# Two of four heads transposed by VectorE and sixteen transfers a group, in groups 2 to 9 of a two-layer graph kernel

## The chip, the core and the metric

One core of one Trainium2 chip. The metric is the device time of one execution in microseconds; the kernel before has a median of 3792.05 over 3 runs (3787.47 to 3802.44).

## What is computed

Two layers over B = 16 graphs of N = 1024 nodes with D = 256 features, each added to its input. The first is attention with 8 heads of 32 features under an adjacency mask, the second weights nodes by edge scores. Cut to what matters:

```python
h = maximum(layernorm(x), 0)
Q, K, V = proj(Wq, bq), proj(Wk, bk), proj(Wv, bv)          # b, 8 heads, 1024, 32
scores = where(adj == 0, -inf, einsum('bhnd,bhmd->bhnm', Q, K) * SCALE)
x = x + einsum('bhnm,bhmd->bhnd', softmax(scores), V) @ Wo.T + bo
h = maximum(layernorm(x), 0)
e_k = leaky_relu(einsum('bid,bjd->bij', h * a_k, h))        # k = 0..3, chosen by adj == k + 1
x = x + einsum('bij,bjd->bid', softmax(where(adj == 1, e_0, ...)), h)
```

## The kernel before

A **tile** is one head's scores of 128 nodes against all 1024: 8 heads x 8 blocks of nodes = 64 tiles a graph, numbered t, and four tiles (four heads of the same nodes) are a **group** g = t // 4, 16 groups a graph. The program has one step a tile, the slot s, and every engine walks the 64 slots of a graph in its own `stage` function; the loop over graphs has graph b's first layer and, between its slots, the second layer of graph b - 1 (its "edge" tiles t = 0..7, from slot 13 on, four slots each) and the front of graph b + 1 (from slot 40). Graph 0 is peeled off and has no second layer beside it. The order is written out by hand: `background` gives for each slot what PE does `ahead` of that slot's transposes and `behind` them, and the other engines read the same lists.

A tile goes through: scores on PE (L1070, two matmuls into `ps`), mask with row minimum on DVE (L754, into `sm`, a ring of three buffers), exponential on ACT (L490), eight 128x128 transposes on PE (L1082, into `pT[0]` and `pT[1]`), and a half copy each on ACT (L501) and DVE (L766) into `pt`, so that the other nodes lie on the partitions. When a group's four tiles are there, the value product (L1095, "av") multiplies them with `v` in 32 matmuls (64 records in the trace), ACT copies the result to `ot` (L511). The lookahead is fixed: PE does the scores of tile s + 3 in slot s, after waiting for the mask of tile s + 1; DVE does the mask of tile s + 2 in slot s, before it copies tile s:

```python
pe.wait_ge(masked, TILES * b + s + 2)      # PE, slot s, then scores(b, s + 3)
behind[HG * g + HG].append(("av", g))      # the value product of group g: slot 4g + 4
```

The second layer uses the same engines: matmuls for edge scores (L1017), masks (L865), leaky ReLU (L873), transposes (L1143), copies (L551, L881), the product (L1152) and the result (L886, L889). SP issues all transfers from one queue, in order: the adjacency halves (L230), which POOL turns into masks, the stores (L274), x (L218, L221) and the "stacks" (L250), which copy 32 partitions of `parts` into `qs` or `ks` of three row blocks, 128 KB each, twelve in a row.

## Time and profile before

| | |
|---|---|
| Median of 3 runs | 3792.05 us (3787.47 to 3802.44) |
| Span of the profiled execution | 3783.3 us; its own time isn't given apart from it |
| PE, PEld | 3454.1 us (91%), 2916.1 us (77%) |
| DVE, ACT, POOL | 75%, 65%, 30% |
| Chain that ended last | PE 61%, issue 11%, ACT 10%, SPq 7%, DVE 7% |
| DMA | 286.63 MB on SP's queue, 27.0% of 16 engines |

PE is the matmul side of TensorE and PEld its weight loads, which overlap; a busy PE is not PE at its peak, since matmuls are pipelined. The chain is followed back from the last instruction to whatever released each step; "issue" is time in which the engine waited for nothing that the profile shows. SPq is SP's queue of DMA instructions.

### The profile page before, as it was taken

The numbers are of one execution on the slowest core, as the hardware profiler recorded it, in microseconds if no ns is written. First come the engines' busy times: TensorE is split into PE (matmuls) and PEld (weight loads), VectorE is DVE, ScalarE is ACT, GpSimd is POOL, SyncE is SP. The second block draws the span as 40 slices with busy tenths as digits, with TensorE's granted clock in tenths as the row PEclk, the third lists the DMA queues.
The fourth block names the chain that finished last, engine by engine and source line by source line (L and its number), as shares of the span: only waits on it lengthen the run. The fifth ranks groups of instructions, "written<-read, shape, count | busy, mean of one in ns | idle before, by whom it ended". The sixth has DMA issues, their size and how long they took to land.

```text
span 3783.3 us, 97534 instructions
## 1 busy us (share of the span) xinstructions
PE 3454.1 (91%) x34096; PEld 2916.1 (77%) x34096; DVE 2850.7 (75%) x5622; ACT 2464.4 (65%) x4548; POOL 1125.2 (30%) x568
## 2 busy tenths in 40 slices
PE   5889999899998999999899998999989999998975
PEld 4678778787787878778787787877878787787864
DVE  4777778787787878878777787878778787887752
ACT  4775767657676676766757676666766757676541
POOL 2232423323232232423323232232422324233212
PEclk8999999999999999999999999999999999999988
DMA  4141412314132141412414132141321414123101
GB/s 120 51 113 54 128 36 81 93 58 122 40 103 72 59 121 55 112 53 67 107 54 128 40 100 75 54 125 49 110 57 56 122 54 128 40 86 89 37 27 44
DMA packets 166740, 294.99 MB, mean 78 GB/s; under 512 B 25536, under 2 KB 75968, under 8 KB 166080
## 3 DMA queue, kind: packets, MB, share of 16 engines
q1 hardware_dynamic: 166080, 286.63, 27.0%
q8 instruction: 361, 5.91, 0.7%
q14 instruction: 299, 2.45, 0.2%
HBM read 169.09 MB, written 16.78 MB: 49 GB/s over the span
## 4 chain that ended last, share of the span: by engine, by line
PE 61%; issue 11%; ACT 10%; SPq 7%; DVE 7%; DMA 2%; POOL 0%; DVEq 0%; ACTq 0%; POOLq 0%
PE pT L1082 15%; PE pG L1017 13%; PE pG L1095 11%; PE pG L1152 8%; PE ps L1070 7%; SPq L250 6%; ACT sm L490 4%; PE pT L1143 3%; PE pG L1051 3%; DMA adj_half<-in_adj_dram 2%; ACT pt L501 2%; DVE sm L754 1%; DVE pt L766 1%; PE pG L1108 1%; ACT sm L546 1%
## 5 line engine op out<-in xcount | busy, mean ns | idle before, releaser
L754 DVE CUSTOM_DVE_ANT_0 sm<-ps,bias 128x1024 f32<-128x1024 f32 x1024 | 1244.1, 1215 | 20.6 <-issue 17.0
L1082 PE MATMUL pT<-ident,sm 128*128 128x128 f32 x8192 | 1099.7, 276 | 127.0 <-ACT pt L501 108.9
L1082 PEld LDWEIGHTS pT<-ident,sm 128*128 128x128 f32 x8192 | 946.5, 141 | 345.0 <-ACT sm L490 140.4
L490 ACT ACTIVATE sm<-sm,mn 128x1024 f32<-128x1024 f32 x1024 | 1180.5, 1153 | 48.5 <-DVE mn L754 48.0
L501 ACT COPY pt<-pT 128x512 f32<-128x512 f32 x1024 | 596.3, 582 | 592.6 <-PE pT L1082 592.4
L766 DVE COPY pt<-pT 128x512 f32<-128x512 f32 x1024 | 703.0, 687 | 287.1 <-PE pT L1082 281.4
L417 POOL TENSOR_SCALAR gbias<-adj_half 128x512 bf16<-128x512 int32 x256 | 505.2, 1973 | 1324.3 <-DVE mn L865 1030.1
L1070 PE MATMUL ps<-ks,qs 96*128 96x512 f32 x2048 | 760.9, 453 | 76.7 <-DVE mn L754 64.1
L400 POOL TENSOR_SCALAR bias<-adj_half 128x512 bf16<-128x512 int32 x256 | 492.5, 1924 | 785.5 <-DMA adj_half<-in_adj_dram 712.0
L1095 PE MATMUL pG<-pt,v 128*32 128x128 f32 x16384 | 530.7, 283 | 27.5 <-DVE x L889 18.5
L1095 PEld LDWEIGHTS pG<-pt,v 128*32 128x32 f32 x16384 | 455.1, 114 | 87.9 <-issue 39.3
L1152 PE MATMUL pG<-h,pt 128*128 128x256 f32 x1920 | 468.6, 379 | 0.0
L1070 PEld LDWEIGHTS ps<-ks,qs 96*128 96x128 f32 x2048 | 350.4, 192 | 146.8 <-DVE mn L754 66.0
L865 DVE CUSTOM_DVE_ANT_0 sm<-pG,gbias 128x512 f32<-128x512 f32 x256 | 176.9, 691 | 280.8 <-PE pG L1017 237.9
L1017 PE MATMUL pG<-hh,parts 128*128 128x512 f32 x1024 | 376.5, 410 | 2.7 <-DVE parts L736 2.7
L1152 PEld LDWEIGHTS pG<-h,pt 128*128 128x128 f32 x1920 | 346.5, 190 | 41.0
L511 ACT COPY ot<-pG 128x128 f32<-128x128 f32 x256 | 68.2, 267 | 353.7 <-PE pG L1095 350.4
L1017 PEld LDWEIGHTS pG<-hh,parts 128*128 128x128 f32 x1024 | 197.4, 193 | 43.2 <-DVE parts L736 3.1
L546 ACT ACTIVATE sm<-sm,mnl 128x1024 f32<-128x1024 f32 x128 | 146.6, 1145 | 92.0 <-DVE mnl L876 90.5
L1017 PE MATMUL pG<-hl,parts 128*128 128x512 f32 x512 | 204.1, 399 | 0.0
L490 ACT ACTIVATION_READ_ACCUMULATOR sm<-sm,mn 128x1 f32 x1024 | 198.5, 194 | 0.0
L1143 PE MATMUL pT<-ident,sm 128*128 128x128 f32 x1024 | 145.4, 287 | 42.2 <-ACT sm L546 37.9
(104 smaller groups left out, 3328.1 us busy)
## 6 DMA issues: line engine op xcount, KB each, us to landing
adj_half<-in_adj_dram SPq DMA_DIRECT2D x512, 256.0 KB, 2.9
ks<-parts SPq DMA_DIRECT2D x384, 128.0 KB, 2.4
qs<-parts SPq DMA_DIRECT2D x384, 128.0 KB, 2.6
x<-in_x_dram SPq DMA_DIRECT2D x16, 1024.0 KB, 5.6
out_dram<-x SPq DMA_DIRECT2D x128, 128.0 KB, 2.6
x<-in_x_dram SPq DMA_DIRECT2D x32, 256.0 KB, 3.5
rb<-in_x_dram SPq DMA_DIRECT2D x16, 256.0 KB, 3.2
sq<-in_x_dram SPq DMA_DIRECT2D x16, 256.0 KB, 3.3
```

Source lines behind the costliest of these rows:

```text
L400: nc.gpsimd.tensor_scalar(bias[:, node, c * HALF:(c + 1) * HALF], adj_half[:, c, :], 0.0, BIG, ALU.is_equal, ALU.mult).then_inc(adj_used[c ...
L417: nc.gpsimd.tensor_scalar(half, adj_half[:, c, :], 0.5, BIG, ALU.is_lt, ALU.mult).then_inc(adj_used[c], 1)
L490: nc.scalar.activation(sm[:, ring(t), :], sm[:, ring(t), :], ACT.Exp, scale=-1.0, bias=mn[:, t:t + 1], accum_out=den[:, t:t + 1]).then_inc ...
L501: nc.scalar.copy(pt[:, place(t), 0:NT // 2, :], pT[0][:, :].rearrange("p (m n) -> p m n", n=P)).then_inc(pt_made[0], 1)
L754: nc.vector.tensor_tensor_reduce(out=sm[:, ring(t), :], in0=ps[t % 2][:, :], in1=bias[:, node, :], scale=1.0, scalar=3e38, op0=ALU.add, op ...
L766: nc.vector.tensor_copy(pt[:, place(t), NT // 2:, :], pT[1][:, :].rearrange("p (m n) -> p m n", n=P)).then_inc(pt_made[1], 1)
L1017: last = nc.tensor.matmul(out, a, c, start=start and i == 0, stop=stop and i == len(terms) - 1)
L1070: last = nc.tensor.matmul(ps[t % 2][:, c * HALF:(c + 1) * HALF], qs[0:ROWS, head, node * P:(node + 1) * P], ks[:, head, c * HALF:(c + 1) * ...
L1082: last = nc.tensor.transpose(pT[c][:, j * P:(j + 1) * P], sm[:, ring(t), m * P:(m + 1) * P], ident[:, :])
L1095: last = nc.tensor.matmul(pG[i][HD * h:HD * (h + 1), 0:P], v[:, m, o:o + HD], pt[:, place(HG * g + h), m, :], start=(m == 0), stop=(m == N ...
L1143: last = nc.tensor.transpose(pT[c][:, j * P:(j + 1) * P], sm[:, RING, m * P:(m + 1) * P], ident[:, :])
L1152: last = nc.tensor.matmul(out[:, 0:D], pt[:, edge_place(t), m, :], h1[:, m, :], start=(m == 0), stop=(m == NT - 1))
```

## The change

In groups 2 to 9 the first two tiles of each group are transposed by DVE in blocks of 32x32 (`turn`, into `turned`), and sixteen transfers of 32 partitions and 64 KB (`swap_blocks`) put the blocks on the right partitions of `pt`. PE's transposes and both half copies of these tiles are gone; for the other two tiles of such a group ACT does both half copies. The value product of these groups stands ahead of the transposes in slot 4g + 6 in place of behind them in slot 4g + 4. The buffer `turned` lies over the projection weights, which four transfers park in unused rows of `ks` and bring back once a graph. Around this, `rows`, `norm`, `result`, some edge transposes and products, and the front's statistics move by a slot or a few. Counters of transposes and copies count only the tiles still done by PE (`PLAIN`). Cut to its core (the pieces stand in the order of the file: tables, `background`, SP's new functions and its `stage`, ACT's `copy`, DVE's `turn` and `stage`, PE's `values` and `stage`):

```diff
+SWAPPED = tuple(range(2, 10))
+BATCH = 4 * 16
+TURNED = tuple(HG * g + h for g in SWAPPED for h in range(2))
+PLAIN = tuple(t for t in range(TILES) if t not in TURNED)
...
     for g in range(1, GROUPS - 1):
-        behind[HG * g + HG].append(("av", g))
+        if g in SWAPPED:
+            ahead[HG * g + HG + 2].append(("av", g))
+        else:
+            behind[HG * g + HG].append(("av", g))
...
+            def swap_blocks(b, g):
+                sp.wait_ge(turn_made, len(TURNED) * b + turned_before(HG * g + 2))
+                settle(sp)
+                sp.wait_ge(av, GROUPS * b + g)
+                settle(sp)
+                for k in range(4):
+                    for a in (0, 2, 1, 3):
+                        c = a ^ k
+                        sp.dma_start(swap[HD * c:HD * (c + 1), :, a, :, :].rearrange("p h m j -> p h (m j)"),
+                                     turned[HD * a:HD * (a + 1), :, c, :, :].rearrange("p h m j -> p h (m j)")
+                                     ).then_inc(swapped[a], 16)
...
-                for t in range(4):
-                    edge_adj(o, t, base)
+                edge_adj(o, 0, base)
+                edge_adj(o, 1, base)
+                swap_blocks(b, 2)
+                swap_blocks(b, 3)
+                edge_adj(o, 2, base)
+                swap_blocks(b, 4)
+                edge_adj(o, 3, base)
+                swap_blocks(b, 5)
                 store(o, 0)
                 edge_adj(o, 4, base)
+                swap_blocks(b, 6)
...
+                if t // HG in SWAPPED:
+                    act.wait_ge(tr[1], len(PLAIN) * b + plain_before(t) + 1)
+                    nc.scalar.copy(pt[:, place(t), NT // 2:, :], pT[1][:, :].rearrange("p (m n) -> p m n", n=P)
+                                   ).then_inc(pt_made[1], 1)
...
+            def turn(b, t, first):
+                dve.wait_ge(exped, TILES * b + t + 1)
+                if t == TURNED[0] and first:
+                    dve.wait_ge(parked, BATCH)
+                if t % HG == 0 and (t > TURNED[0] or not first):
+                    for a in range(4):
+                        dve.wait_ge(swapped[a], BATCH * (len(SWAPPED) * b + SWAPPED.index(t // HG)))
+                settle(dve)
+                nc.vector.transpose(turned[:, t % HG, :, :, :].rearrange("p c m j -> p m c j"),
+                                    sm[:, ring(t), :].rearrange("p (m c j) -> p m c j", m=NT, c=4)
+                                    ).then_inc(turn_made, 1)
...
-                    copy(b, s, not earlier)
+                    if s in TURNED:
+                        turn(b, s, not earlier)
+                    elif s // HG not in SWAPPED:
+                        copy(b, s, not earlier)
...
+                if g in SWAPPED:
+                    for a in range(4):
+                        pe.wait_ge(swapped[a], BATCH * (len(SWAPPED) * b + SWAPPED.index(g) + 1))
...
+                        if HG * g + h in TURNED:
+                            moving = swap[:, h, :, m, :]
...
-                    transposes(b, s, not earlier)
+                    if s not in TURNED:
+                        transposes(b, s, not earlier)
```

Three places in the order of the instructions. First DVE in graph 0, slots 15 to 18, before: each slot has a mask (`sm,mn<-ps,bias`) and a half copy; the reciprocal and L777 are row factors, L787 is a norm.

```order
L773 RECIPROCAL rden<-den 128x16 [waits exped]
L777 SCALAR_TENSOR_TENSOR rb<-mn,rden 128x512 [waits f_tr,r_tr,r_rec]
L754 ISA sm,mn<-ps,bias 128x1024 [waits s_mm,tr1]
L754 ISA mn 128x1
L766 COPY pt<-pT 128x512 [waits av,tr1]
L754 ISA sm,mn<-ps,bias 128x1024 [waits s_mm,tr1]
L754 ISA mn 128x1
L787 TENSOR_TENSOR ot<-pG,ot 128x512 [waits r_tr,o_copied]
L766 COPY pt<-pT 128x512 [waits av,tr1]
L754 ISA sm,mn<-ps,bias 128x1024 [waits tr1,adj_used1,s_mm,adj_used0]
```

And DVE in the same slots of the changed program, where tiles 16 and 17 are the first two of group 4.

```order
L896 RECIPROCAL rden<-den 128x16 [waits exped]
L900 SCALAR_TENSOR_TENSOR rb<-mn,rden 128x512 [waits f_tr,r_tr,r_rec]
L864 ISA sm,mn<-ps,bias 128x1024 [waits s_mm,tr1]
L864 ISA mn 128x1
L877 STREAM_TRANSPOSE turned<-sm 128x8x4x32 [waits swapped2,swapped3,swapped1,exped,swapped0]
L864 ISA sm,mn<-ps,bias 128x1024 [waits s_mm,turn_made]
L864 ISA mn 128x1
L877 STREAM_TRANSPOSE turned<-sm 128x8x4x32 [waits exped]
L864 ISA sm,mn<-ps,bias 128x1024 [waits turn_made,adj_used1,s_mm,adj_used0]
```

The half copies are gone; in their place stand two transposes, of which the first waits for the transfers of the group before (`swapped0` to `swapped3`), with the mask of tile 19 behind it. The norm has moved behind a later copy.

Second, PE in graph 0, one group, before: scores (`ps<-ks,qs`) and transposes (`pT<-ident,sm`) in turn, the value product (`pG<-pt,v`) once a group.

```order
L1095 MATMUL pG<-pt,v 32x128 x32
L1070 MATMUL ps<-ks,qs 128x512 x2
L1082 MATMUL pT<-ident,sm 128x128 x8
L1070 MATMUL ps<-ks,qs 128x512 x2
L1082 MATMUL pT<-ident,sm 128x128 x8
L1070 MATMUL ps<-ks,qs 128x512 x2
L1082 MATMUL pT<-ident,sm 128x128 x8
L1070 MATMUL ps<-ks,qs 128x512 x2
L1082 MATMUL pT<-ident,sm 128x128 x8
L1095 MATMUL pG<-pt,v 32x128 x32
```

And a changed group.

```order
L1235 MATMUL pG<-pt,v 32x128 x32
L1215 MATMUL pT<-ident,sm 128x128 x8
L1203 MATMUL ps<-ks,qs 128x512 x2
L1215 MATMUL pT<-ident,sm 128x128 x8
L1203 MATMUL ps<-ks,qs 128x512 x6
L1235 MATMUL pG<-pt,v 32x128 x32
```

Two of four sets of transposes are gone, and the scores of three tiles (x6) stand in a row ahead of the value product, each behind its wait for a mask.

Third, SP in the loop over graphs: between two waits for adjacency halves (`adj_half`) there was nothing or a store.

```order
L230 ISA [waits adj_used1]
L230 DMA adj_half<-in_adj_dram 128x512
L236 ISA
L225 REGISTER_ALU [waits g_sel]
L230 ISA [waits adj_used0]
L230 DMA adj_half<-in_adj_dram 128x512
```

Now:

```order
L277 ISA [waits adj_used1]
L277 DMA adj_half<-in_adj_dram 128x512
L329 REGISTER_ALU
L331 REGISTER_ALU [waits turn_made]
L336 DMA pt<-turned 32x2x256 [waits av]
L336 DMA pt<-turned 32x2x256 x15
```

Sixteen transfers stand behind a wait for the second transpose of their group and for the value product of the group before.

## Rows read from the trace of the kernel before

**Rows 1.** The page, busy time and share of the span by engine.
```profile
PE 3454.1 (91%) x34096; PEld 2916.1 (77%) x34096; DVE 2850.7 (75%) x5622; ACT 2464.4 (65%) x4548; POOL 1125.2 (30%) x568
```

**Rows 2.** Chain of waits, graph 6, one group: start us, us, what.
```profile
1457.91 1.88 PE pG L1095 x64
...
1460.82 0.46 PE ps L1070 x2
...
1462.67 0.87 PE pT L1082 x8
...
1472.40 1.88 PE pG L1095 x64
```

**Rows 3.** Value products 2 and 9 of graph 6, chain of waits, then of graph 0, timeline.
```profile
1430.25 1.88 PE pG L1095 x64
...
1532.68 2.00 PE pG L1095 x64
...
94.26 1.96 PE L1095 MATMUL pG<-pt,v 128*32 128x128 f32 x64
...
162.62 2.01 PE L1095 MATMUL pG<-pt,v 128*32 128x128 f32 x64
```

**Rows 4.** DVE and ACT: costliest groups of the page, then DVE's timeline, graph 6.
```profile
L754 DVE CUSTOM_DVE_ANT_0 sm<-ps,bias 128x1024 f32<-128x1024 f32 x1024 | 1244.1, 1215 | 20.6 <-issue 17.0
L501 ACT COPY pt<-pT 128x512 f32<-128x512 f32 x1024 | 596.3, 582 | 592.6 <-PE pT L1082 592.4
L766 DVE COPY pt<-pT 128x512 f32<-128x512 f32 x1024 | 703.0, 687 | 287.1 <-PE pT L1082 281.4
...
1485.47 0.15 DVE L886 RECIPROCAL rden<-den 128x1 f32<-128x1 f32 x1
...
1486.06 1.21 DVE L754 CUSTOM_DVE_ANT_0 sm<-ps,bias 128x1024 f32<-128x1024 f32 x1
...
1491.87 0.69 DVE L865 CUSTOM_DVE_ANT_0 sm<-pG,gbias 128x512 f32<-128x512 f32 x1 [1.34 <-PE pG L1017]
```

**Rows 5.** SP's queue: durations (ns min/median/max) and landing by line, timeline, the page's queues.
```profile
L250 SPq DMA_DIRECT2D qs<-parts x384: 507/592/2372, 46.4 to 3437.4; - x192
DMA to landing us min/median/max: 2.3/2.4/4.8
L230 SPq DMA_DIRECT2D adj_half<-in_adj_dram x510: 327/333/1552, 33.2 to 3761.0; - x170
L274 SPq DMA_DIRECT2D out_dram<-x x128: 332/356/1200, 312.3 to 3780.4; - x128
...
0.73 0.46 SPq L207 DMA_DIRECT2D x<-in_L_gnn_Wq_dram  x1
1.25 0.45 SPq L207 DMA_DIRECT2D x<-in_L_gnn_Wk_dram  x1
4.74 2.01 SPq L215 DMA_DIRECT2D acol<-in_L_gnn_a_dram  x4
38.59 7.59 SPq L250 DMA_DIRECT2D ks<-parts  x12
1570.57 8.38 SPq L250 DMA_DIRECT2D ks<-parts  x12
q1 hardware_dynamic: 166080, 286.63, 27.0%
```

**Rows 6.** Timeline of graph 6: a result on DVE and the store that waits for it.
```profile
1485.66 0.48 DVE L889 SCALAR_TENSOR_TENSOR x<-pG,rden,x 128x256 f32<-128x256 f32 x1
1486.37 0.35 SPq L274 DMA_DIRECT2D out_dram<-x  x1
```

**Rows 7.** Windows: us, PE, PEld, DVE, ACT, POOL busy (x), granted clock, DMA share, GB/s.
```profile
170.00:200.00 30.00, 20.52 (x221) 16.93 (x222) 16.33 (x28) 18.63 (x37) 7.69 (x4) 0.83 0.22 71
1470.00:1500.00 30.00, 30.00 (x286) 26.21 (x286) 23.00 (x49) 18.35 (x35) 7.84 (x5) 1.00 0.14 47
3700.00:3780.00 80.00, 51.27 (x197) 42.06 (x196) 21.50 (x55) 9.13 (x15) 19.22 (x10) 0.81 0.13 44
```

More of the change, by code:

```diff
@@ L37, with plain_before, turned_before, rows_slot @@
 NORM = {5: (0, 1, 2, 3), 6: (4, 5), 7: (6, 7)}
+def plain_before(t):
+    return sum(1 for p in PLAIN if p < t)
+def turned_before(t):
+    return sum(1 for p in TURNED if p < t)
+def rows_slot(quad):
+    return 16 * quad + (17 if 4 * quad + 3 in SWAPPED else 16)
+def result_slot(t):
+    return EDGE + 1 + 4 * NT if t == NT - 1 else EDGE + (8 if t in LATE else 7) + 4 * t
 def background(earlier, later):
@@ L63, in background @@
         for t in range(NT):
-            behind[EDGE + 4 + 4 * t].append(("sum", t))
+            behind[EDGE + (5 if t in LATE or t == SPARED else 4) + 4 * t].append(("sum", t))
     if later:
@@ L125, in two_graph_layers @@
         xf = [x1[:, 0:2, :], x1[:, 2:4, :]] + [part[:, :].rearrange("p (t d) -> p t d", d=D) for part in (rb, sq)]
-        wqh, wql = sb("wqh", [P, KT, D], R), sb("wql", [P, KT, D], R)
-        wkh, wkl = sb("wkh", [P, KT, D], R), sb("wkl", [P, KT, D], R)
+        with nc.sbuf_tensor("turned", [P, 2, 4, NT, HD], F) as turned:
+            pass
+        wqk = sb("wqk", [P, 4 * KT * D], R)
+        wqh, wql, wkh, wkl = (wqk[:, i * KT * D:(i + 1) * KT * D].rearrange("p (k d) -> p k d", k=KT)
+                              for i in range(4))
+        swap = pt[:, 0:2, :, :].rearrange("p h m n -> p h (m n)").rearrange("p h (a m j) -> p h a m j", a=4, m=NT)
         wvh, wvl = sb("wvh", [P, KT, D], R), sb("wvl", [P, KT, D], R)
@@ L593, in stage @@
                         edge_copy(o, NT - 1)
+                    edge = (s - EDGE - 3) // 4 if earlier and EDGE + 3 <= s < EDGE + 3 + 4 * NT and s % 4 == 0 else None
+                    if edge in LATE:
+                        edge_exp(o, edge)
                     if s + 1 < TILES:
@@ L919, in stage @@
                 for s in range(TILES):
-                    if earlier and EDGE + 7 <= s < EDGE + 3 + 4 * NT and (s - EDGE) % 4 == 3:
-                        t = (s - EDGE - 7) // 4
-                        result(o, t, pG[bank("sum", t)])
+                    for t in range(NT - 1):
+                        if earlier and s == result_slot(t):
+                            result(o, t, pG[bank("sum", t)])
                     if s + 2 < TILES:
@@ L944, in stage @@
                             evacuate(kind, n)
-                    copy(b, s, not earlier)
+                    if s in TURNED:
+                        turn(b, s, not earlier)
+                    elif s // HG not in SWAPPED:
+                        copy(b, s, not earlier)
+                    for quad in range(QUADS - 1):
+                        if s == rows_slot(quad) + 1 and 4 * quad + 3 in SWAPPED:
+                            norm(b, quad, bank("rows", quad))
                     for kind, n in behind[s]:
@@ L1031, in qk @@
                 pe.wait_ge(f_l, 4 * f + 2 * (n % 2) + 2)
+                if back and n == 0:
+                    pe.wait_ge(w_back, BATCH * f)
                 o = slice((q // 2) * P, (q // 2 + 1) * P)
@@ L1094, in values @@
                         o = (HG * hg + h) * HD
[L1095 to L1096 removed]
+                        if HG * g + h in TURNED:
+                            moving = swap[:, h, :, m, :]
+                        else:
+                            moving = pt[:, place(HG * g + h), m, :]
+                        last = nc.tensor.matmul(pG[i][HD * h:HD * (h + 1), 0:P], v[:, m, o:o + HD], moving, start=(m == 0), stop=(m == NT - 1))
                 last.then_inc(av, 1)
@@ L1244, in stage @@
[L1244 to L1252 removed]
+                        product(kind, n, len(PLAIN) * b + plain_before(s))
@@ new lines, in stage @@
+                    for t in range(NT):
+                        if earlier and s == EDGE + (5 if t in LATE else 4) + 4 * t:
+                            pe.wait_ge(lpt[0], NT * o + t + 1)
+                            pe.wait_ge(lpt[1], NT * o + t + 1)
+                    if s not in TURNED:
+                        transposes(b, s, not earlier)
+                    for t in range(NT - 1):
+                        if earlier and s == EDGE + (7 if t in LATE else 6) + 4 * t:
+                            edge_values(o, t, pG[bank("sum", t)], (1, 2, 3) if t == SPARED else (2, 3))
@@ new lines, in stage @@
+                    for kind, n in behind[s]:
+                        product(kind, n, len(PLAIN) * b + plain_before(s + 1))
+                    if earlier and EDGE + 3 <= s < EDGE + 3 + 4 * NT and s % HG == 0:
+                        pe.wait_ge(pt_made[0], len(PLAIN) * b + plain_before(s + 1))
+                        pe.wait_ge(pt_made[1], len(PLAIN) * b + plain_before(s + 1))
+                        edge_transposes(o, (s - EDGE - 3) // 4)
+                    for t in range(NT - 1):
+                        if earlier and s == EDGE + (6 if t in LATE else 5) + 4 * t and t != SPARED:
+                            edge_values(o, t, pG[bank("sum", t)], (1,))
```

145 lines of the change are left out of this document (88 added, 57 removed).

## The prediction

> **What bounds the kernel now.** I read the page's engine line first [rows 1]: PE is busy 91% of the span, VectorE (DVE) 75%, ScalarE (ACT) 65%. A share says little about one stage, so I went on to the chain of waits inside one turn of the loop over graphs [rows 2]. There the reader sees PE follow PE without a gap: from one value product (L1095) to the next, 1457.91 to 1472.40, is 14.5 us, and four groups of eight transposes (L1082) stand in it, 0.87 us each on the chain. Nothing else ends last in that stretch, so PE work taken away there is time won, until another loop becomes longer.
>
> For the length of a group of four tiles I take value products 2 and 9, the first and last of the eight groups that change; seven periods lie between. In graph 6, which stands for the 15 graphs that carry the second layer of the graph before, they start at 1430.25 and 1532.68: 102.4 / 7 = **14.6 us** a group. In graph 0, without a second layer, 94.26 to 162.62: 68.4 / 7 = **9.8 us** [rows 3].
>
> **What PE, ACT and DVE get back.** Of eight groups two tiles each lose their eight PE transposes: 2 x 0.87 = 1.75 us of PE a group [rows 2]. ACT loses four half copies (two tiles, both engines had one half each) and takes over DVE's two for the other tiles: from 4 x 0.59 to 4 x 0.59 us, nothing. DVE loses four half copies of 0.69 us and gets two transposes of a 128x1024 tile. No row shows such a transpose; the nearest are passes of the same size, 1.22 us [rows 4], and I take that. Bounds: 0.7 us (a pass over half of it), and 2.4 us (two passes). DVE is then even to 0.3 us better a group, with room in either case. The Trainium skill, "VectorE: DVE Perf Modes", section on the three transpose paths, gives 311 ns for a 128x128 bf16 block and recommends TensorE where the result is a whole 128x128 transpose; eight such blocks would be 2.5 us, by which each period worked out below would be 1.3 to 2.6 us longer. No run here shows it. The value product now reads its moving tile in pieces of 32 elements; I price that at nothing, since no row separates it, and let the range carry it. Moving av by two tiles costs PE nothing by itself: PE does the same work in another order, and the ot copy and the row factors that follow have a group's time.
>
> **What is added: a loop that goes around once a group.** This is where the sum is decided, and the order of waits says it. Sixteen transfers of group g may be issued only when av(g-1) is done, since it reads the one placed buffer. All sixteen must have landed before DVE may do the first transpose of group g+1, since that overwrites the one turned buffer. DVE runs in order: behind that transpose stand the mask of tile 4g+7 and the second transpose. PE runs in order too: before av(g) it waits for that mask. And av(g), with the second transpose, lets SP start on group g+1. No part of it overlaps the next turn, as every buffer on it is single. Its length:
>
> 1. Issue. Fifteen spacings c between issues. The nearest rows are SP's other SBUF to SBUF transfers of 32 partitions, the stacks: 12 in 7.59 us, the last one 0.59 long, so (7.59 - 0.59) / 11 = 0.636 us a spacing [rows 5]. They move 128 KB each and the new ones 64 KB. I take **c = 0.635**: 9.5 us. That it is a matter of issue and not of bytes is my choice, for two reasons in rows: even a stack that found the queue idle took 0.507 us, where loads and stores of 128 and 256 KB take 0.33 to 0.36; and landing stays at 2.3 to 2.4 us for the median, so nothing piles up [rows 5]. Bounds: 0.33 + 0.03, the issue of a load that stands alone; and 0.70, since a burst of 12 inside the loop took 8.38 us [rows 5].
> 2. Landing of the last: 2.4 us [rows 5].
> 3. From there to the release of SP. By PE: transpose 1.2, reciprocal and result of the second layer 0.6 (1485.47 to 1486.06, where the next mask begins), mask 1.2, the scores ahead of av 0.5, av 1.9, and 0.3 for its last matmul to drain: 5.7. By DVE: transpose, result, mask, the edge copy and the edge mask at 0.6 each between starts, transpose: 5.3. I take 5.7; in graph 0, without the second layer's pieces, 5.1 [rows 2, 4].
> 4. Handovers between engines: a result ends at 1486.14 and SP's store, which waits for it, begins 0.23 us later [rows 6]. Two of the loop's handovers are to SP or from its transfers, two between DVE and PE, which I take to be short: 0.5 in all.
>
> Sum: 9.5 + 2.4 + 5.7 + 0.5 = **18.1 us** for a period that now takes 14.6, and 17.5 in graph 0 where it takes 9.8. So the 1.75 us that PE gets back buys nothing in these groups: PE would be ready after 12.9 and waits about 5 for the mask. In other words the change replaces an engine bound of PE by a latency bound with SP's issue as its largest term, and everything that PE, ACT and POOL do is cover for it.
>
> SP's other work: the adjacency loads, stores and loads of x between the batches (some 0.4 to 1 us each) stand where SP waits for the turn or for av anyway; I price them at nothing, and if a load's wait for POOL is late, the batch behind it slips by as much. The bytes (1 MB a group, 128 groups, 134 MB on top of 287) find the DMA engines at a share of 27% [rows 5]; nothing. Parking the weights is four transfers once, and bringing them back four a graph, with more than a group of slack before the first projection; nothing. If that slack is gone, the cost is one landing a graph.
>
> **The sum.** Second-layer graphs: (18.1 - 14.6) x 7 x 15 = +367. Graph 0: (17.5 - 9.8) x 7 = +54. The eighth group, before the loop closes and after it opens, keeps its saving of 1.75: x 16 = -28. Together +393 on a span of 3783.3: 4176. Around the span lie 8.8 us to the median of the runs, 3792.05 (the profile's own time isn't given apart from it), so the forecast is **4185 us**, about 10% slower.
>
> **Rivals.**
>
> *Issue as fast as in the other bursts (slower, but less).* The first loads of the program follow each other at 0.51 us, whether their rows have 1 KB (0.73 to 1.25) or 4 bytes (acol: 4 in 2.01) [rows 5]. If that pace holds whatever the ends of the transfer are, c = 0.5 and the period is 16.1: 1.5 x 105 + 5.7 x 7 - 28 = +170, **3962 us**. For it: the new transfers carry half the stacks' bytes. Against it: the 0.507 of an idle stack. The Trainium skill, "SBUF — State Buffer", section on the DMA setup-cost knee, has a loop of 64 KiB transfers at about 138 GB/s and so speaks against many small ones; sixteen are 7.6 us by it, an estimate of c = 0.475, and the total would be some 3925.
>
> *Bytes, not issue, set the stacks' pace (faster).* 128 KB in 0.635 us is 206 GB/s. If the queue was held up by its bytes, 64 KB take 0.32 and the issue alone decides, 0.32 to 0.36 as for a lone load [rows 5]. Then the period is 5.1 + 8.6 = 13.7: 0.9 x 105 = -95, graph 0 (13.1 - 9.8) x 7 = +23, -28: -100, **3692 us**. This is one mechanism, and it decides at c = (14.6 - 8.6) / 15 = 0.40: under it the change gains, down to PE's own 12.9 a group. For it: the stacks' median of 592 ns is near their 507 at best, as even as a rate of bytes would be. Against it: bursts of loads with almost no bytes in them keep 0.51 and not 0.36. The same page's section on the DMA port swizzle says that 32 partitions reach 8 of 16 ports, about 218 GB/s; the row's 206 agrees with it, and by that rule alone this rival would be the likeliest.
>
> *PE loses its clock (slower still).* Today PE runs at 2.4 GHz nearly throughout; where it waits more, the granted clock falls: 1.00 in a full stretch of graph 6, but 0.83 in 170 to 200 with PE busy 68%, and 0.81 in the tail at 64% [rows 7]. In the new period PE is busy about 12.9 of 18.1, and right behind its wait stand the scores and av, 2.3 us, on the loop. If they ran at 1.2 GHz in every other period, +2.3 x 112 / 2 = +129, **4314 us**; in every one, 4443.
>
> *Nothing measurable:* c near 0.4, and the gain and loss cancel. It needs a value between two rows that have nothing there.
>
> **Chances.** Forecast (c from 0.57 to 0.70, clock mostly kept) 0.55; the 0.5 pace 0.21; the clock 0.13; the byte limit 0.08; nothing 0.03. Slower by over 0.5% (19 us, about what a measurement tells from no change) is 0.55 + 0.21 + 0.13 = 0.89, faster 0.08, within 0.03. The range holds the forecast with c up to 0.70 (+1.0 x 112 = 4297), most of the clock's case, and the 0.5 case down to 3940: **3940 to 4350**.
>
> **What the profile would show.** Right: value products 2 to 9 of a middle graph about 18 us apart; PE's busy share near 80%; idle time before the scores, put down to the mask; before DVE's first transpose of a group, put down to a DMA; the new transfers about 0.6 us apart on SP, and SP's queue in the chain with a fifth of the span or more; a transpose on DVE at 1.2 us. Wrong: transfers under 0.45 us apart, periods at 14 or less, or DVE transposes of 2 us and more, which would make DVE's branch the longer one. If the periods are 18 but the total is not up by 350, the groups outside the eight gave something back that I don't see.

## The result and the profile after

The changed kernel takes **4448.2 us** (median of 4 runs, 4434.3 to 4450.6) where the one before took 3792.9 (median of 4, 3787.5 to 3802.4): ratio 1.172, 95% interval 1.170 to 1.175. The forecast was 4185 with a range up to 4350, so the direction was right and the size was not: of +655 us, +393 had been foreseen. The span of the profiled execution is 4445.5 us against 3783.3, its mean granted TensorE clock 0.895 against 0.974.

The page of the changed kernel, busy time by engine, beside [rows 1]:
```profile
PE 3518.0 (79%) x32048; PEld 2869.8 (65%) x32048; DVE 2824.1 (64%) x5366; ACT 2447.7 (55%) x4548; POOL 1113.4 (25%) x568
```
PE has 2048 matmuls fewer and is busy 64 us longer: the same work took more time each. PE's share is close to the 80% that the prediction asked for. Its other sign, SP's queue in the chain with a fifth of the span, can't be read: the chain on this page accounts for some 4% of the span in all.

What DVE and PE wait for (view of waits: engine, line, what for, us in total, times, longest), SP's sixteen transfers (duration in ns, min/median/max, then landing in us) and DVE's transpose (the same columns):
```profile
DVE turned L877 <- DMA pt<-turned: 520.7, 112, 8.9
PE ps L1203 <- DVE mn L864: 519.3, 212, 10.8
PE ps L1070 <- DVE mn L754: 64.1, 72, 3.9
...
L336 SPq DMA_DIRECT2D pt<-turned x2048: 585/597/2047, 89.0 to 4237.7; - x187
DMA to landing us min/median/max: 2.0/2.0/4.1
...
L877 DVE STREAM_TRANSPOSE turned<-sm x256: 1233/1241/1247, 85.0 to 4223.6; 128x1024 f32<-128x1024 f32 x128
```
The third line is the kernel before. The 112 waits of DVE for a transfer are the first transposes of groups 3 to 9 in 16 graphs: seven a graph, one for each turn of the loop after the first. The scores (L1203) stand behind the mask (L864), as the loop says. The transpose takes 1.24 us, where the forecast took 1.2 from a pass of the same size [rows 4]; the 2.5 us that the Trainium skill's figure for 128x128 bf16 blocks would have given, by the forecast's estimate from eight blocks ("VectorE: DVE Perf Modes", section on the three transpose paths), is not what this trace shows.

One whole turn in graph 6, from value product 2 to value product 3 (timeline: start us, us, engine, line, operation; in brackets idle time before it and what ended it), with SP's row from a look at its queue alone:
```profile
1705.24 3.60 PE L1235 MATMUL pG<-pt,v 128*32 128x128 f32 x64
1708.98 10.19 SPq L336 DMA_DIRECT2D pt<-turned  x16
1720.88 1.25 DVE L877 STREAM_TRANSPOSE turned<-sm 128x1024 f32<-128x1024 f32 x1 [4.25 <-DMA pt<-turned]
1722.32 1.22 DVE L864 CUSTOM_DVE_ANT_0 sm<-ps,bias 128x1024 f32<-128x1024 f32 x1 [0.19 <-DVE turned L877]
1723.60 0.73 PE L1203 MATMUL ps<-ks,qs 96*128 96x512 f32 x2 [2.90 <-DVE mn L864]
1724.07 0.68 DVE L988 CUSTOM_DVE_ANT_0 sm<-pG,gbias 128x512 f32<-128x512 f32 x1
1725.10 3.10 PE L1235 MATMUL pG<-pt,v 128*32 128x128 f32 x64 [0.77 <-DVE mn L988]
```
Read downwards: the value product releases SP, the landing of SP's last transfer the transpose, the transpose the mask, and the mask the scores. The edge mask (L988) stands on DVE behind the mask and an edge copy, and the next value product, ready after its scores, waits 0.77 us for it. The parts against the forecast's: from the value product's start to SP's first transfer 3.74 us (1.9 + 0.3 + a handover); from there to the transpose 11.90 (9.5 + 2.4 = 11.9, and a handover); to the mask 1.44 (1.2); to the scores 1.28 (1.2); to the value product 1.50, of which 0.77 is that wait for the edge mask (0.5). In this turn no second-layer result stands on the loop. The sum is 19.86.

The value products 1, 9 and 10 of graph 6 (product 2 is the first row above), then 1, 2 and 9 of graph 0, beside [rows 3]. Where a row has fewer than 64 matmuls, the window ends inside the product or other work lies between them:
```profile
1682.11 1.08 PE L1235 MATMUL pG<-pt,v 128*32 128x128 f32 x32 [1.03 <-ACT pt L600]
...
1842.87 0.86 PE L1235 MATMUL pG<-pt,v 128*32 128x128 f32 x24
1842.87:1854.62 11.75, 10.77 (x115) 9.04 (x114) 7.37 (x15) 9.73 (x19) 3.86 (x2) 1.00 0.60 130
...
84.09 0.42 PE L1235 MATMUL pG<-pt,v 128*32 128x128 f32 x8 [0.41 <-DVE pt L889]
104.81 1.08 PE L1235 MATMUL pG<-pt,v 128*32 128x128 f32 x16
...
237.47 1.43 PE L1235 MATMUL pG<-pt,v 128*32 128x128 f32 x21 [2.85 <-DMA pt<-turned]
```
(The third row is the window from product 9 to product 10, with the columns of [rows 7].) The seven periods of graph 6 are (1842.87 - 1705.24) / 7 = 19.7 us against 14.6, those of graph 0 (237.47 - 104.81) / 7 = 18.95 against 9.8. The period before them, which the forecast left out, is 23.1 us where it was 12.4; the one behind is 11.8 where it was 14.8.

### The profile page after: what moved, and what is told of

The parts are those of the page before. It is cut to its first block and busy times, and to the rows that moved or that the text cites. A ratio compares the mean times of both kernels' runs of the same rounds, so it can differ in the third digit from the quotient of the medians.

```text
span 4445.5 us, 96851 instructions
## 1 busy us (share of the span) xinstructions
PE 3518.0 (79%) x32048; PEld 2869.8 (65%) x32048; DVE 2824.1 (64%) x5366; ACT 2447.7 (55%) x4548; POOL 1113.4 (25%) x568
## 5 line engine op out<-in xcount | busy, mean ns | idle before, releaser
L864 DVE CUSTOM_DVE_ANT_0 sm<-ps,bias 128x1024 f32<-128x1024 f32 x1024 | 1246.0, 1217 | 65.6 <-DVE turned L877 32.8
L1203 PE MATMUL ps<-ks,qs 96*128 96x512 f32 x2048 | 792.3, 470 | 525.9 <-DVE mn L864 519.3
L600 ACT COPY pt<-pT 128x512 f32<-128x512 f32 x768 | 446.1, 581 | 904.4 <-PE pT L1215 808.2
L1215 PE MATMUL pT<-ident,sm 128*128 128x128 f32 x6144 | 843.1, 281 | 89.9 <-ACT pt L600 67.6
L1215 PEld LDWEIGHTS pT<-ident,sm 128*128 128x128 f32 x6144 | 720.8, 144 | 259.7 <-ACT pt L600 101.2
L1203 PEld LDWEIGHTS ps<-ks,qs 96*128 96x128 f32 x2048 | 358.3, 202 | 645.8 <-DVE mn L864 607.5
L1235 PE MATMUL pG<-pt,v 128*32 128x128 f32 x16384 | 666.8, 329 | 48.3 <-ACT pt L600 15.4
L1235 PEld LDWEIGHTS pG<-pt,v 128*32 128x32 f32 x16384 | 567.1, 133 | 168.2 <-issue 116.9
L877 DVE STREAM_TRANSPOSE turned<-sm 128x1024 f32<-128x1024 f32 x256 | 318.0, 1242 | 520.7 <-DMA pt<-turned 520.7
L889 DVE COPY pt<-pT 128x512 f32<-128x512 f32 x512 | 351.3, 686 | 223.8 <-PE pT L1215 178.1
L988 DVE CUSTOM_DVE_ANT_0 sm<-pG,gbias 128x512 f32<-128x512 f32 x256 | 176.0, 688 | 406.9 <-PE pG L1148 359.6
L1291 PE MATMUL pG<-h,pt 128*128 128x256 f32 x1680 | 414.8, 383 | 0.0
L1291 PEld LDWEIGHTS pG<-h,pt 128*128 128x128 f32 x1680 | 313.9, 193 | 45.4
L1282 PE MATMUL pT<-ident,sm 128*128 128x128 f32 x1024 | 154.1, 300 | 89.8 <-ACT sm L649 63.8
L1282 PEld LDWEIGHTS pT<-ident,sm 128*128 128x128 f32 x1024 | 129.5, 154 | 118.4 <-issue 72.4
```

Source lines behind the costliest of these rows:

```text
L600: nc.scalar.copy(pt[:, place(t), 0:NT // 2, :], pT[0][:, :].rearrange("p (m n) -> p m n", n=P)).then_inc(pt_made[0], 1)
L864: nc.vector.tensor_tensor_reduce(out=sm[:, ring(t), :], in0=ps[t % 2][:, :], in1=bias[:, node, :], scale=1.0, scalar=3e38, op0=ALU.add, op ...
L877: nc.vector.transpose(turned[:, t % HG, :, :, :].rearrange("p c m j -> p m c j"), sm[:, ring(t), :].rearrange("p (m c j) -> p m c j", m=NT ...
L889: nc.vector.tensor_copy(pt[:, place(t), NT // 2:, :], pT[1][:, :].rearrange("p (m n) -> p m n", n=P)).then_inc(pt_made[1], 1)
L1203: last = nc.tensor.matmul(ps[t % 2][:, c * HALF:(c + 1) * HALF], qs[0:ROWS, head, node * P:(node + 1) * P], ks[0:ROWS, head, c * HALF:(c + ...
L1215: last = nc.tensor.transpose(pT[c][:, j * P:(j + 1) * P], sm[:, ring(t), m * P:(m + 1) * P], ident[:, :])
```

## The experiments

Each is the changed kernel with one edit, unless it says otherwise. "Period" is the time from one value product to the next, the median over the middle graphs where several are meant, worked out from the rows of the value products in the trace. The kernel before was run beside every experiment, with medians from 3791.2 to 3800.8 us, so a difference of some 10 us between two experiments says little.

**half_bytes**: the same sixteen transfers with 32 KB in each; half of the placed data is left out.
```diff
-    sp.dma_start(swap[HD*c:HD*(c+1), :, a, :, :]..., turned[HD*a:HD*(a+1), :, c, :, :]...)
+    sp.dma_start(swap[HD*c:HD*(c+1), :, a, 0:NT//2, :]..., turned[HD*a:HD*(a+1), :, c, 0:NT//2, :]...)
```


> Leaves out half of each transfer: sixteen transfers a group of 32 partitions but 32 KB. Loop theory with a fixed issue cost: spacing stays at 0.60 to 0.64 us, total 4400 to 4450 (only the landing of the last shorter, by 0.1 to 0.2). Rival, bytes over few ports set the pace: spacing 0.32, 4.8 us less in each of 112 periods, about 3910.

4406.0 us (one run). The same piece of graph 6, timeline:
```profile
1685.84 3.36 PE L1235 MATMUL pG<-pt,v 128*32 128x128 f32 x64
1689.34 10.19 SPq L336 DMA_DIRECT2D pt<-turned  x16
...
1705.32 2.04 PE L1235 MATMUL pG<-pt,v 128*32 128x128 f32 x41 [0.76 <-DVE mn L988]
```
The burst takes 10.19 us, the same as with twice the bytes: (10.19 - 0.6) / 15 = 0.64 us a transfer is issue, not data. That is the forecast's c = 0.635. The landing is 0.1 us shorter in the median (1.9 against 2.0), and the total 42 us below the changed kernel, inside the band expected. The rival in which bytes set the pace is out. The Trainium skill's section on the DMA port swizzle ("SBUF — State Buffer") gives some 218 GB/s for 32 partitions; 32 KB in 0.64 us are 51 GB/s, so that ceiling is not what spaces the transfers here.

**four_wide**: four transfers of 128 partitions and 256 KB in place of the sixteen. They don't move blocks across partitions, so the value product reads wrong blocks; bytes and order are the same.
```diff
-    for k in range(4): for a in (0, 2, 1, 3): ... 32 partitions each
+    for a in range(4): sp.dma_start(swap[:, :, a, :, :]..., turned[:, :, a, :, :]...)
```


> Leaves the placement out: four transfers of 128 partitions and 256 KB (same bytes a group, same buffers, same waits) in place of sixteen of 32 partitions, so blocks land on the wrong partitions. Loop theory with a fixed issue cost a transfer (0.64 us): the period of about 20 us in the changed groups falls by 12 x 0.64 = 7.7 to about 12.4, under the 14.6 that PE had before, so PE bounds again with 1.75 us a group less: 3570 to 3680. Rival, issue cost grows with bytes: spacing 2.5 us, period unchanged, 4400 to 4500. Rival, the new cost lies in the transposes or in the value product's moving tile, not in the transfers: 4300 to 4450.

3766.5 us (one run): the loop is gone, and a transfer of 256 KB takes SP 0.63 us in the median, as one of 64 KB does. But of the expected gain over the kernel before, 112 to 222 us, only some 26 came. The period before the changed groups' first product is still 17.4 us where it was 12.4, and the next 14.8 where it was 12.4. **four_wide_ot** asks why.
```diff
+    for kind, n in ahead[s] + behind[s]:          # ACT, in slot s
+        if kind == "av" and n in SWAPPED: high(kind, n)
     if s not in TURNED: copy(b, s, not earlier)   # and no second time behind it
```


> Like four_wide (four transfers of 128 partitions in place of the sixteen: they put the blocks in wrong partitions, so the output is not the reference's, but the bytes are the same), and ACT copies the value product out before it copies the tile of the same slot, where four_wide does it behind. In four_wide the groups with nothing in PE's way took 12.7 us, and others 14.7, where PE waits 1.7 us for DVE's sum of ot, which waits for ACT's copy of the value product, which stands behind two copies of a tile. Theory (with the value product two tiles later, this copy is late and holds the gain back): the wait goes, the periods of 14.7 come to 13.0 to 13.3, about 4 x 1.5 x 15 = 90 us: 3660 to 3700. Rival (the wait moves to the next late thing on the same bank, the edge mask): under 25 us, 3740 to 3770.

3722.3 us (one run), between the theory's band and the rival's. Windows from one value product to the next (columns of [rows 7]), first four_wide, two periods, then four_wide_ot, one; behind them PE's wait in four_wide:
```profile
1456.39:1471.10 14.71, 13.02 (x125) 10.93 (x125) 10.60 (x20) 8.42 (x15) 3.69 (x2) 1.00 0.35 110
1471.10:1483.84 12.74, 12.74 (x125) 10.89 (x125) 10.78 (x21) 8.68 (x17) 3.84 (x2) 1.00 0.41 136
...
1482.23:1496.92 14.69, 13.69 (x129) 11.25 (x129) 12.72 (x27) 9.03 (x18) 4.00 (x3) 1.00 0.41 129
...
PE pG L1146 <- DVE ot L908: 50.7, 30, 1.7
```
PE full for 12.74 us is the 12.9 that the forecast named as PE's own bound: here the saving of eight transposes twice is seen whole, against 14.5 before. It comes only in some groups. In two others of each graph PE waits 1.7 us for the sum of ot, behind ACT's copy of the value product, and the saving is given back; with that copy earlier, those two periods are 1.5 to 1.6 us shorter and the total 44 us. So the value product's later place was not free. The rest (the 14.69 window, where DVE has 12.72 to do) stays where the second layer's pieces are.

**group_9**: `SWAPPED = (9,)`, one changed group a graph.

> Only group 9 is changed, groups 2 to 8 as before. Loop theory: the loop needs two changed groups next to each other; a lone one has a whole graph's time for its transfers and saves its 1.75 us of PE: 3793 - 28 = 3765, 0.7% faster than before. Rival, each changed group costs something of itself ((4448 - 3793) / 128 = 5.1 us): 3875, 2% slower. A late value product that waits for its own transfers would show as up to 3 us a graph, 3840.

3760.9 us, ratio 0.992, interval 0.989 to 0.994. The total is as the theory had it, and the rival's 3875 is out: nothing of the next group waits for the sixteen transfers. But the periods say that the theory's number came by luck. Value products 8 and 9 of graph 6, then PE's scores of the fourth tile of the next graph, in the kernel before and in group_9 (timelines):
```profile
1500.23 1.95 PE L1236 MATMUL pG<-pt,v 128*32 128x128 f32 x64 [1.68 <-DVE x L1013]
1520.33 1.95 PE L1236 MATMUL pG<-pt,v 128*32 128x128 f32 x64
...
1610.20 1.19 PE L1070 MATMUL ps<-ks,qs 96*128 96x512 f32 x2 [3.33 <-DVE mn L754]
...
1590.97 0.70 PE L1204 MATMUL ps<-ks,qs 96*128 96x512 f32 x2
```
The period before product 9 is 20.1 us where it was 14.9, and the one behind it 11.8 where it was 14.8: around the changed group the kernel **loses** some 2 us a graph, 32 us over 15 graphs. The span is 34 us shorter all the same, because other periods give back more: the one ahead of a graph's last product alone 44 us. There PE waited 3.1 to 3.9 us before those scores in 11 of 16 graphs of the kernel before, and in group_9 it does not wait. No tile near it is turned by DVE, and the other variants that were traced have that gain too. Which of the other pieces that the change moves brings it is not shown: the kernel with those moves and no changed group was not run.

**groups_6_9**: `SWAPPED = tuple(range(6, 10))`.

> Groups 6 to 9 alone are changed. Theory (the loop is paid between neighbours only, three times a graph, and the last group pays nothing and saves PE's transposes): group 9 alone stood at 224.4 us a graph; the periods 6 to 7, 7 to 8 and 8 to 9 come to what they are with all eight changed (20.7, 20.1, 18.1 in place of 15.2, 15.8 and 20.1, which is 7.8 more) and the one before, 5 to 6, is longer by what the later value product adds, some 5: 237 us a graph, 3950 to 3990. Rival (the cost is the same for each changed group, neighbour or not: (4448 - 3793) / 8 = 82 us each): 4120.

4043.7 us (one run), over the theory's band and under the rival's 4120: both missed. Timeline, value product 5 and what follows:
```profile
1573.55 1.96 PE L1236 MATMUL pG<-pt,v 128*32 128x128 f32 x64 [0.38 <-DVE x L1013]
...
1580.70 11.26 SPq L337 DMA_DIRECT2D pt<-turned  x16
1593.68 1.25 DVE L878 STREAM_TRANSPOSE turned<-sm 128x1024 f32<-128x1024 f32 x1 [7.62 <-DMA pt<-turned]
```
Product 6 comes at 1597.84, 24.3 us after 5. The three periods between changed groups are 20.4, 19.9 and 18.1, near what was expected (20.7, 20.1, 18.1); the miss is the first one, 24.2 where 14.5 stood before and some 5 more were expected. Product 6 stands, in PE's order, behind the mask of tile 31, and that mask behind the first transpose of group 7 (the last row), which waits for group 6's own transfers. So **the first group of a run pays a full turn too**, on top of its two tiles' delay. The forecast had counted seven turns for eight groups; this is the "eighth" it priced at a gain.

**groups_2_9**: `SWAPPED = (2, 9)`, with tile 3 of group 2 in place 4.

> Only groups 2 and 9 are changed (each has the time of several groups for its sixteen transfers; tile 3 of group 2 goes to place 4 and not 3, since its neighbours keep their first tile in 3). Theory (what a changed group costs is the loop alone, and without a changed neighbour each saves PE's two times eight transposes): group 9 alone gave -32 us, so twice that: 3725 to 3745. Rival (group 2, right behind the start of the graph, has no time to spare, because the value product of group 2 two tiles later meets the row factors or the ot copies): 3755 to 3775, as with group 9 alone, or worse.

3815.5 us, ratio 1.006, interval 1.004 to 1.008: slower than before, and 55 us slower than group 9 alone. The theory fell; it is the rival's "or worse". The period before product 2 is 19.3 us where it was 12.4. Group 2, timeline, and the window from product 1 to 2 (columns of [rows 7]):
```profile
1434.41 10.74 SPq L338 DMA_DIRECT2D pt<-turned  x16
1446.72 1.95 PE L1237 MATMUL pG<-pt,v 128*32 128x128 f32 x64 [1.88 <-DMA pt<-turned]
...
1427.72:1446.72 19.00, 12.99 (x131) 9.84 (x132) 14.99 (x25) 13.79 (x26) 1.92 (x1) 1.00 0.33 85
1417.81:1430.18 12.37, 10.52 (x121) 8.02 (x121) 10.51 (x17) 10.54 (x21) 0.00 (x0) 1.00 0.14 44
```
The last row is the same stretch of the kernel before. PE had 10.5 of 12.4 us to do there: it was not full, so its saving buys nothing, and the transfers end 1.9 us after PE is ready for them even with no neighbour changed.

**warm** and **warm_30**: idle transposes of the identity into `pT[0]`, on PE, where it waits for the mask. Warm makes 44, and in group 9 they write over a tile that `pT[0]` holds; warm_30 makes 30 and none in group 9.
```diff
+    if earlier and s % HG == 2 and g in SWAPPED[:-1] and g - 3 in range(NT):   # g = s // HG - 1
+        pe.wait_ge(lpt[0], NT * o + g - 3 + 1)
+        for _ in range(WARM): nc.tensor.transpose(pT[0][:, 0:P], ident[:, :], ident[:, :])
```


> PE does 44 idle transposes of the identity (4.8 us at full clock) where it waits for the mask ahead of the late value product, in groups 3 to 9 with a second layer beside. Clock theory: the granted clock stays at 1, the value product behind the wait takes 1.95 us and not 3.1 to 3.6, the scores 0.73 and not 1.2: 1.3 to 1.9 us less in each of 105 periods, 4250 to 4310. Rival, the clock falls in places that are off the loop (DVE's branch to the second transpose is as long): 4400 to 4450. If the idle transposes run past the mask, slower than 4448.

> The changed kernel with 30 idle 128-column transposes of the identity on PE in the second-layer groups 3 to 8 (not 9), once a group, where PE has run out of work and waits for the mask; nothing is left out of the result. In the trace of the changed kernel, the 7 periods whose value product ran in 1.95 us took 18.3 us on average and the 34 with one of 3.6 us or more took 20.3. Theory (the loop is as forecast and the rest of the miss is PE's clock): the value product back at 1.95 us, these periods at 18.0 to 18.6, about -1.4 x 6 x 15 = -125 us: 4300 to 4350. Rival (the slow value product is not on the loop, its length goes with something else that is late): value product at 1.95, periods still 19.5 or more, 4430 to 4460.

Warm: 4533.2 us, ratio 1.195 (1.191 to 1.198). The product came back to 1.95 us, but 44 transposes ran past the mask and came onto the loop. Warm_30: 4425.4, ratio 1.166 (1.163 to 1.168), 23 us under the changed kernel where 98 to 148 were expected. Timeline of warm_30, graph 6, value products 3 and 4, then the end of the turn before product 7:
```profile
1721.02 1.96 PE L1236 MATMUL pG<-pt,v 128*32 128x128 f32 x64 [0.40 <-DVE mn L989]
1735.18 3.44 PE L1371 MATMUL pT<-ident 128*128 128x128 f32 x30
1739.40 1.95 PE L1236 MATMUL pG<-pt,v 128*32 128x128 f32 x64
...
1795.41 1.11 PE L1248 MATMUL pG<-ident,rb 128*128 128x128 f32 x4 [3.27 <-DVE x L1013]
1796.32 4.62 PE L1371 MATMUL pT<-ident 128*128 128x128 f32 x30
1801.33 0.86 PE L1236 MATMUL pG<-pt,v 128*32 128x128 f32 x24
```
In the first turn the product is back at 1.96 us and the period is 18.4, where the changed kernel has 19.9 at the same place. In the second, PE came to the idle work late, behind a wait for a result (L1013), so that the work, 4.6 us long, fell onto the loop: the period before product 7 is 23.9 there instead of 20.7. And the product came back to 1.95 us in only 62 of the 90 turns, never that of group 5. So the total is no measure, but the periods are. In warm_30 the 62 that begin with a product of 1.95 us took 18.6 us. In the changed kernel the 7 that begin with one of 1.95 us took 18.3 and the 35 with one of 3.6 or more 20.3. These lie at different places of the graph. At the same place, changed kernel against a run with the product back: 19.9 and 18.4 from 3 to 4, 19.9 and 19.0 from 4 to 5, 20.1 and 18.9 from 7 to 8, 18.1 and 16.5 from 8 to 9 (warm_30), and 20.6 and 18.3 from 5 to 6 (warm). **The clock is worth 0.9 to 2.3 us a turn, about 1.5 in the mean.** The product alone says much the same: over the 105 turns it takes 3.31 us in the mean, 1.36 more than 1.95.

**split_act**: half of the transfers issued by ACT.
```diff
-    for a in (0, 2, 1, 3):     # SP
+    for a in (0, 2):           # SP; a in (1, 3) is issued by ACT in slot 4g+2, with the same waits
```


> Of the sixteen transfers eight (source quarters 1 and 3) are issued by ACT in slot 4g+2, behind its copies of the value product, and eight stay on SP; nothing else changes. Theory (each transfer costs its issuing queue 0.64 us, and two queues issue side by side): the issue term falls from 15 to 7 spacings, -5.1 us, unless ACT comes late to it; the period then is bound near ACT's own work, 9 busy + 8 x 0.6 issue = 14, so 14.5 to 16 and the kernel 3830 to 4000. Rival (the queues share what generates the descriptors): both together still take 0.64 us a transfer, the period stays at 19 to 20, 4400 to 4500.

4135.7 us, ratio 1.092 (1.089 to 1.095). Timeline, one turn:
```profile
1637.79 5.24 SPq L336 DMA_DIRECT2D pt<-turned  x8
1638.86 0.59 ACTq L613 DMA_DIRECT2D pt<-turned  x1
1639.48 4.52 ACTq L613 DMA_DIRECT2D pt<-turned  x7
1644.12 1.15 ACT L589 ACTIVATE sm<-sm,mn 128x1024 f32<-128x1024 f32 x1 [4.58 <-issue]
```
Two queues issue side by side, each at some 0.65 us a transfer, so the cost is a queue's own, and the rival in which both together still take 0.64 us is out. But ACT's next exponential starts only after 4.58 us of issuing, and that comes onto the path in its place: 16.1 to 18.4 us a period, not 14.5 to 16, and a total 136 us over the theory's band.

**split_pool** gives that half to POOL instead; **split_pool_2** mends one order in it: POOL makes both halves of a graph's first edge bias before its transfers of group 2, since SP waits for that bias's buffer ahead of its own.
```diff
     for c in range(2):
-        if c == 1 and swaps: swap_others(o + 1, t + 2)          # POOL, split_pool
+        if c == 1 and swaps and t: swap_others(o + 1, t + 2)    # split_pool_2; for t == 0 behind the loop
```


> As split_act, but the second eight transfers are issued by POOL, between the two halves of its edge bias, in place of ACT; the row factor for the next graph moves behind the last of them. In split_act SP issued 8 in 5.24 us and ACT 8 beside them, but ACT stood still for 4.6 us over it and its exponentials came late: 17.1 to 17.3 us a period. Theory (a queue on an engine with room gives the whole of the 5.1 us; what ACT took away was its own time): periods of 14 to 15.5, POOL busy but not late, 3790 to 3900. Rival (POOL, whose transfers no row has shown, issues more slowly than SP, over 1 us each): periods of 17 to 20, 4150 to 4450.

> As split_pool, but POOL makes both halves of the first edge bias of a graph before its eight transfers of group 2, where they stood between the halves. In split_pool SP's own eight of group 2 began at 1516.51, 7 us after POOL's (1509.40), because SP waited with the load of the next adjacency for that half, and the two first periods took 24.9 and 17.3 us, all others 13.3 to 16.5. Theory (only that order stood in the way, and with it gone the loop costs nothing): first periods of 17.5 and 14.5 to 15 as in four_wide, about -9.5 x 15 = -140 us: 3800 to 3850. Rival (the entry into the changed groups costs its turn of the loop in any order): 3930 to 3970.

3965.8 us, ratio 1.045 (1.043 to 1.048), between the theory's band and the rival's, and 3857.6, ratio 1.016 (1.011 to 1.020), just over its theory's. POOL's and SP's rows in split_pool, the first turn of a graph (SP's last row runs on into the next group's eight), then in split_pool_2, one turn:
```profile
1509.40 4.31 POOL L514 DMA_DIRECT2D pt<-turned  x8 [15.30 <-DVE turned L895]
1503.08 13.17 SPq L277 DMA_DIRECT2D adj_half<-in_adj_dram  x2
1516.51 19.58 SPq L336 DMA_DIRECT2D pt<-turned  x16
```
```profile
1478.39 5.10 SPq L336 DMA_DIRECT2D pt<-turned  x8
1479.02 4.28 POOL L514 DMA_DIRECT2D pt<-turned  x8 [1.95 <-PE pG L1255]
```
In split_pool SP starts group 2 at 1516.51, 7.1 us behind POOL, and the two first periods take 24.9 and 17.3 us; mended, 18.5 and 17.0. Behind them stand 14.7, 13.2, 14.2, 15.1, 15.7 and 16.5, against 19.8 to 20.7 and 18.1 with one queue. The mend gave 108 us where 115 to 165 were expected: the second period (17.0, not 14.5 to 15) is not settled.

**split_pool_ot** adds ACT's early copy to split_pool_2, **split_pool_3_9** leaves group 2 unchanged besides (`SWAPPED = tuple(range(3, 10))`).

> As split_pool_2, and ACT copies the value product out before the tile copies of the slot. Theory (as four_wide_ot against four_wide, -44 us): -30 to -50 us against split_pool_2, 3760 to 3815. Rival (with eight transfers on each of two queues the loop still ends last and the copy has time): within 15 us of split_pool_2.

> As split_pool_ot, but group 2 stays as before. In groups_2_9 against group_9 the change of group 2 cost 55 us, since DVE and ACT and not PE are full at the start of a graph. Theory: -55 to -80 us against split_pool_ot, 3700 to 3750, under group 9 alone (3758). Rival (the entry cost moves on to group 3): no change against split_pool_ot.

3828.9 us, ratio 1.008 (1.005 to 1.010), and **3752.0**, ratio 0.987 (0.983 to 0.992). Both steps came near their theories, 29 us for the copy (expected 30 to 50) and 77 for group 2 (55 to 80), though both totals lie above their bands, by 14 and 2 us. The kernel with seven changed groups and two queues is faster than before, but here too not by its changed groups: against the kernel before, the span is 33 us shorter, and the periods ahead of and behind a graph's last product alone are 65 us shorter, so everything else is 32 us longer. Value products 3 and 4 of graph 6 in split_pool_3_9:
```profile
1449.42 1.95 PE L1261 MATMUL pG<-pt,v 128*32 128x128 f32 x64 [0.78 <-DVE mn L1014]
...
1462.63 1.95 PE L1261 MATMUL pG<-pt,v 128*32 128x128 f32 x64
```
That is a period of 13.2 us with the product at full clock. **group_9_ot**, the early copy with group 9 alone, gave no more than group 9:

> Group 9 alone changed, and ACT copies its value product out before the two half copies of the tile of the same slot. With group 9 alone: 3761 us, ratio to before 0.9916. In four_wide_ot the earlier copy gave 44 us over seven or eight changed groups, about 0.35 us a group and graph. Theory: PE's wait for DVE's sum of ot (1.7 us, once a graph here) goes in part: 3740 to 3757. Rival (behind group 9 PE has other work, and the wait is not on its path): 3757 to 3765, no difference that can be told.

3758.0 us, ratio 0.991 (0.989 to 0.992), inside its rival's band. The best kernel found is split_pool_3_9, 49 us under the runs of the kernel before beside it (3800.8); its interval overlaps group 9's, so that it beats that one is not shown; nor is it shown that either beats a kernel with the moved pieces and no changed group.

## Why the forecast was wrong

*What bounds the kernel before* was right where it was read, in the middle of a graph: PE alone, 14.5 us a group, and 12.74 once its two times eight transposes are gone (four_wide). For group 2 it was not: PE has 10.5 of 12.4 us there, and I had taken graph 6's middle for all eight groups.

*The loop* was right in its parts and its mechanism. Issue to transpose measured 11.90 us against 11.9; spacing 0.64 against 0.635; landing 2.0 against 2.4; transpose 1.24 against 1.2. With the product at 1.95 us the period is 18.3 to 18.6 in the mean against 18.1; the wait for the edge mask had no term. Single groups (group_9), fewer issues (four_wide) and two queues (split_pool_2) each take it away, half the bytes (half_bytes) do not.

*The clock is the step that failed first.* It stood among the rivals at 0.13, and the forecast said "clock mostly kept". Two turns read as follows, in graph 6 (columns of [rows 7]), then the scores and the value product at the start of the first:
```profile
1705.24:1725.10 19.86, 13.59 (x113) 10.79 (x113) 10.94 (x21) 8.74 (x17) 3.59 (x3) 0.83 0.32 80
1804.71:1824.81 20.10, 16.31 (x125) 13.42 (x125) 11.95 (x24) 8.13 (x15) 3.68 (x2) 0.84 0.45 117
...
1704.09 1.22 PE L1203 MATMUL ps<-ks,qs 96*128 96x512 f32 x2 [5.36 <-DVE mn L864]
...
1705.24:1708.84 3.60, 3.60 (x66) 3.03 (x66) 1.79 (x3) 0.07 (x1) 1.52 (x1) 0.53 0.02 7
```
The granted clock is 0.83 to 0.84 over a turn, and it is low where it hurts. After 5.36 us of waiting the product runs at 0.53, near the 1.2 GHz level, and takes 3.60 us instead of 1.95; most take 3.1 to 3.6. The row that should have decided was in [rows 7]: PE busy 68% at a clock of 0.83. The new period has PE busy 12.9 of 18.1, 71%, and I gave that row to a rival. The rival's price for every period (+2.3) was too high: the scores take 1.22 us in only 52 of the 105 turns and some 0.73 in the others. That its total, 4443, lies beside the result is luck, owed to the next term.

*The eighth group was the second.* "The eighth group ... keeps its saving of 1.75" is wrong: the first group of the run pays a turn of the loop and its delay (+10.8 us in the middle graphs, +11.3 in graph 0). Some 5 of the 10.8 come without the sixteen transfers (four_wide, 17.4 against 12.4). The periods around it give back 3.1 us behind group 9, 1.1 ahead of product 1 and 4.0 before the last product of a graph, which group_9 shows to be no doing of the turned tiles. Added up over the whole trace, everything outside the seven periods is 64 us longer, where the forecast had it 28 shorter. Within it "moving av by two tiles costs PE nothing by itself" failed too: it delays product 2 by two tiles, and elsewhere makes PE wait for ot.

*The sum by what was measured.* Graph 0 is 74 us longer, the 14 middle graphs 539 together (38.5 each), the last graph 47 up to its last product, and what stands before and behind 2: the span's 662. By the forecast's terms: the seven periods of the 15 graphs +533 where it had 367, those of graph 0 +64 where it had 54, the rest +64 where it had -28. Of the first difference, 166, the clock is 1.5 x 7 x 15 = 158 by the estimate above; in graph 0 the value products take 3.54 us in the mean, which covers the 10 of the second.

*The other rivals.* Bytes as the limit: out by half_bytes, and by four_wide from the other side. A pace of 0.5 us: no burst of SP shows it (POOL's queue issues at 0.54), and the 7.6 us that the forecast estimated for sixteen transfers from the Trainium skill's "SBUF — State Buffer", section on the DMA setup-cost knee, are 10.2 measured. The pure "nothing measurable" case: out.

## What to carry to other kernels

A single buffer that is written by one engine, moved by DMA and read by another is a loop; write down its length and the number of its turns, and count the first use in a row of neighbours as a turn too. Here a transfer between SBUF buffers cost its queue some 0.6 us with 32, 64, 128 or 256 KB in it, so sixteen small ones on one queue are a latency, and a second queue on an engine with little to do nearly halves it (eight in 5.1 us here). TensorE, when made to wait, may come back at half its clock, on the very instruction that the loop hangs on (0.53 granted in the product behind the wait of 5.36 us): price the work right behind a new wait at both speeds. And look where in the trace a gain lies before crediting it to the edit: a change that also moves other pieces needs a run with those moves alone.

## What was not expected of the hardware

- The bytes left the pace of issue as it was: 16 transfers of 32 partitions take 10.19 us with 64 KB and with 32 KB in each, and four of 128 partitions with 256 KB take 2.64 us. Queues of SP, ACT and POOL issue side by side (medians 0.60, 0.62 and 0.53 us); on ACT that time is the engine's own, 4.58 us for eight.
- PE's clock was down after the waits of each turn (2.9 and 5.4 us before the scores in the rows above), with PE busy 68% of the turn's window, and 30 idle transposes of 3.4 us in that wait gave the product its 1.95 us back in 62 of 90 turns; 44 of them did so in every turn.
- DVE waits 0.19 us between a transpose and the mask behind it (32.8 us over 170 times): the profile names DVE as its own releaser there. The forecast had no term for it.
